# Values' top and remainder side by side in the first attention's loop

## What is computed

```python
q = (xn @ w_q).reshape(B, SQ, 16, 64)
kv = context @ w_kv
k, v = jnp.split(kv, 2, axis=-1)            # each (B, 12544, 16, 64)
scores = jnp.einsum('bqhd,bkhd->bhqk', q * SCALE, k)
attn = jax.nn.softmax(scores, axis=-1)
out = jnp.einsum('bhqk,bkhd->bqhd', attn, v).reshape(B, SQ, 1024)
out = out @ w_out + b_out
return out * jnp.tanh(gate[0])
```

## Time and profile before

| | |
|---|---|
| median of 3 runs | 1176.95 us (1174.17 to 1177.15) |
| profiled execution, its own time | 1175.05 us |
| profiled execution, its span | 1173.3 us |
| busy: PE, DVE, ACT, POOL | 1138.9, 889.1, 901.3, 583.9 us |
| L923, first and last start | 34.6 and 891.9 us |

### The profile page before, as it was taken

How to read it: one execution, slowest core, us unless ns; L and a number is a source line. 1 busy time by engine, 2 the same in 40 slices (tenths; PEclk the granted TensorE clock), 3 DMA queues, 4 the chain that set the end, 5 groups by cost and what they waited for, 6 DMA issues and landing times.

```text
span 1173.3 us, 32542 instructions
## 1 busy us (share of the span) xinstructions
PE 1138.9 (97%) x12748; PEld 814.0 (69%) x12749; DVE 889.1 (76%) x1718; ACT 901.3 (77%) x1552; POOL 583.9 (50%) x548
## 2 busy tenths in 40 slices
PE   8999999999999999999999999999997899889998
PEld 6566666666666666666666666666666758767898
DVE  7777878888888888888878787878774659788632
ACT  5699988889988889898888888889884278586010
POOL 5355656565655565665656565656564070043000
PEclk9999999999999999999999999999999999999999
DMA  5465544445354545354545454544443995150385
GB/s 223 107 183 149 153 116 119 127 95 154 90 154 96 150 92 157 90 154 95 148 95 142 107 138 110 137 108 93 123 92 97 382 341 167 33 180 1 109 285 176
DMA packets 141142, 163.31 MB, mean 139 GB/s; under 512 B 18320, under 2 KB 127280, under 8 KB 140992
## 3 DMA queue, kind: packets, MB, share of 16 engines
q1 hardware_dynamic: 139904, 157.20, 48.0%
q10 hardware_dynamic: 1088, 4.06, 0.9%
HBM read 71.60 MB, written 12.99 MB: 72 GB/s over the span
## 4 chain that ended last, share of the span: by engine, by line
PE 85%; DVE 6%; ACT 4%; issue 2%; DMA 1%; SPq 1%; POOL 0%; DVEq 0%; ACTq 0%; POOLq 0%
PE ps L900 21%; PE ps L872 21%; PE ps L938 7%; PE ps L914 7%; PE ps L2353 4%; PE ps L957 4%; PE ps L955 4%; PE ps L956 4%; PE ps L1681 3%; PE ps L2361 2%; PE ps L1108 2%; ACT ss_decay L1936 2%; PE ps L2135 1%; DMA k_st<-k_rest 1%; PE ps L2117 1%
## 5 line engine op out<-in xcount | busy, mean ns | idle before, releaser
L468 POOL TENSOR_TENSOR pT_lo<-p_exp,pT_hi 128x896 f16<-128x896 f32 x223 | 420.8, 1887 | 313.9 <-ACT pT_hi L580 313.9
L561 ACT ACTIVATE p_exp<-ps,ln_k,esc 128x896 f32<-128x896 f32 x224 | 246.0, 1098 | 54.7 <-PE ps L938 47.1
L693 DVE TENSOR_REDUCE tile_max<-ps 128x128 f16<-128x896 f32 x224 | 244.4, 1091 | 49.6 <-PE ps L914 47.2
L580 ACT ACTIVATE pT_hi<-p_exp 128x896 f16<-128x896 f32 x224 | 211.8, 946 | 1.0
L688 DVE TENSOR_TENSOR v_lo<-ps,v_hi 128x512 f16<-128x512 f32 x196 | 135.4, 691 | 68.6 <-ACT v_hi L553 66.2
L956 PE MATMUL ps<-v_lo,pT_hi 128*128 128x64 f16 x1568 | 164.4, 193 | 0.0
L955 PE MATMUL ps<-v_hi,pT_hi 128*128 128x65 f16 x1568 | 164.3, 193 | 0.1
L957 PE MATMUL ps<-v_hi,pT_lo 128*128 128x65 f16 x1568 | 163.8, 193 | 0.0
L900 PE MATMUL ps<-c_hi,wk_hi 128*128 128x448 f16 x448 | 158.5, 354 | 0.8 <-DVE k_rest L708 0.5
L900 PE MATMUL ps<-c_hi,wk_lo 128*128 128x448 f16 x448 | 157.9, 352 | 0.0
L900 PE MATMUL ps<-c_lo,wk_hi 128*128 128x448 f16 x448 | 157.8, 352 | 0.0
(11 more groups left out here) (406 smaller groups left out, 2074.8 us busy)
## 6 DMA issues: line engine op xcount, KB each, us to landing
k_st<-k_top SPq DMA_DIRECT2D x444, 112.0 KB, 2.3
k_st<-k_rest SPq DMA_DIRECT2D x444, 56.0 KB, 2.0
xa_cn<-in_ctx SPq DMA_DIRECT2D x14, 896.0 KB, 7.5
me_w<-in_me_w SPq DMA_DIRECT2D x8, 1536.0 KB, 6.3
c_raw<-in_ctxT SPq DMA_DIRECT2D x13, 896.0 KB, 5.6
ctx_parts<-c_hi SPq DMA_DIRECT2D x14, 448.0 KB, 3.3
ctx_parts<-c_lo SPq DMA_DIRECT2D x14, 448.0 KB, 2.8
me_w<-in_me_w SPq DMA_DIRECT2D x8, 768.0 KB, 5.9
```

The costliest lines, as they stand in the source:

```text
L468: nc.gpsimd.tensor_tensor(pT_lo[:, n % 2, :, :].rearrange("p t s -> p (t s)"), p_exp[:, n % 2, :], pT_hi[:, n % 2, :, :].rearrange("p t s ...
L561: nc.scalar.activation(p_exp[:, n % 2, :], s_scores[n % 2], ACT.Exp, bias=ln_k[:, 0:1], scale=esc[:, n // H0 % 2:n // H0 % 2 + 1]).then_in ...
L580: nc.scalar.activation(pT_hi[:, n % 2, :, :].rearrange("p t s -> p (t s)"), p_exp[:, n % 2, :], ACT.Copy).then_inc(pT_hi_ready, 1)
L693: nc.vector.tensor_reduce(tile_max[:, n % 2, :], s_scores[n % 2].rearrange("p (t s) -> p s t", s=S), AX.X, ALU.max).then_inc(tile_max_done, 1)
```

## The change

`v_hi` and `v_lo` become one tensor `v_pair`: for each tile and head 64 columns of remainders, 64 of tops, and the ones. `weigh` multiplies `pT_hi` by all 129 columns in one matmul, and `pT_lo` by the last 65 in a second; the third is gone. A head's sum now takes 129 columns of PSUM, so four heads fill the end of bank 6 and the beginning of bank 7, and there is one such place in the stead of two. `flush` has a third operation, which adds the columns of the remainders after the tops, and stands ahead of `v_low` and `tiles_max` in all four steps. `weigh` of the first head of a group waits for the flush of the whole group before (`flushed`), not of the one before that. The transposed maxima go to other columns, without a wait for a flush. The quarters of the next chunk's split move: on ACT from steps 2, 3, 5, 6 to 1, 2, 4, 6, on DVE from 3, 4, 6, 7 to 2, 3, 6, 8 (in chunk 0 ACT keeps its steps, and DVE has 3, 4, 6, 8). SP loads `c_raw` in step 9.

```diff
-VW = DH + 2
+VW = 2 * DH + 2
+V_LO, V_HI = slice(0, DH), slice(DH, 2 * DH)
+PV = 2 * DH + 1
+FLUSH = 3
...
-C_SPLIT_STEPS = (2, 3, 5, 6)
+C_HIGH_STEPS, C_HIGH_FIRST = (1, 2, 4, 6), (2, 3, 5, 6)
+C_LOW_STEPS, C_LOW_FIRST = (2, 3, 6, 8), (3, 4, 6, 8)
...
-        s_pv = [ps[:, b, 0:4 * (DH + 1)].rearrange("p (h e) -> p h e", e=DH + 1) for b in (7, 6)]
+        s_pv = flat[:, 7 * 512 - 2 * PV:7 * 512 + 2 * PV].rearrange("p (h e) -> p h e", e=PV)
...
-                if h == 8 and c + 2 < NCH:
+                if h == 9 and c + 2 < NCH:
                     sp.wait_ge(c_lo_ready, 4 * (c + 2))
                     sp.dma_start(c_raw[:, :, :], ctxT[:, :, (c + 2) * CH:(c + 3) * CH]).then_inc(raw_loaded, 16)
...
-                if h in C_SPLIT_STEPS and c + 1 < NCH:
-                    c_high(c + 1, C_SPLIT_STEPS.index(h))
+                steps = C_HIGH_STEPS if c else C_HIGH_FIRST
+                if h in steps and c + 1 < NCH:
+                    c_high(c + 1, steps.index(h))
...
-                nc.vector.scalar_tensor_tensor(out=acc[:, 4 * g:4 * g + 4, 0:DH], in0=s_pv[g % 2][:, :, 0:DH],
-                                               scalar=v_unscale[:, c % 2:c % 2 + 1], in1=acc[:, 4 * g:4 * g + 4, 0:DH],
-                                               op0=ALU.mult, op1=ALU.add).then_inc(flushed, 1)
-                nc.vector.tensor_tensor(acc[:, 4 * g:4 * g + 4, DH:DH + 1], acc[:, 4 * g:4 * g + 4, DH:DH + 1],
-                                        s_pv[g % 2][:, :, DH:DH + 1], ALU.add).then_inc(flushed, 1)
+                grp = acc[:, 4 * g:4 * g + 4, :]
+                nc.vector.scalar_tensor_tensor(out=grp[:, :, 0:DH], in0=s_pv[:, :, V_HI], scalar=v_unscale[:, c % 2:c % 2 + 1],
+                                               in1=grp[:, :, 0:DH], op0=ALU.mult, op1=ALU.add).then_inc(flushed, 1)
+                nc.vector.tensor_tensor(grp[:, :, DH:DH + 1], grp[:, :, DH:DH + 1],
+                                        s_pv[:, :, 2 * DH:PV], ALU.add).then_inc(flushed, 1)
+                v.wait_ge(flushed, FLUSH * f + 1)
+                nc.vector.scalar_tensor_tensor(out=grp[:, :, 0:DH], in0=s_pv[:, :, V_LO], scalar=v_unscale[:, c % 2:c % 2 + 1],
+                                               in1=grp[:, :, 0:DH], op0=ALU.mult, op1=ALU.add).then_inc(flushed, 1)
                 if c == NCH - 1:
                     hs = slice(4 * g, 4 * g + 4)
-                    v.wait_ge(flushed, 2 * f + 2)
+                    v.wait_ge(flushed, FLUSH * f + FLUSH)
...
+                if h % 4 == 1 and n > 1:
+                    flush(n // 4 - 1)
                 if n and v_at(n - 1):
                     v_low(*v_at(n - 1))
-                if h % 8 == 1 and n > 1:
-                    flush(n // 4 - 1)
                 if n + 2 < NT:
                     tiles_max(n + 2)
-                if h % 8 == 5:
-                    flush(n // 4 - 1)
                 if n + K_AHEAD < NT:
                     k_low(n + K_AHEAD)
-                if h - 1 in C_SPLIT_STEPS and c + 1 < NCH:
-                    c_low(c + 1, C_SPLIT_STEPS.index(h - 1))
+                steps = C_LOW_STEPS if c else C_LOW_FIRST
+                if h in steps and c + 1 < NCH:
+                    c_low(c + 1, steps.index(h))
...
                 if h % 4 == 0:
-                    at_least(pe, flushed, 2 * (c * 4 + h // 4 - 1))
+                    at_least(pe, flushed, FLUSH * (c * 4 + h // 4))
...
-                to = s_pv[h // 4 % 2][:, h % 4, :]
+                to = s_pv[:, h % 4, :]
                 for tile in range(TILES):
                     ph, pl = pT_hi[:, n % 2, tile, :], pT_lo[:, n % 2, tile, :]
-                    nc.tensor.matmul(to, ph, v_hi[:, tile, h, 0:DH + 1], start=(tile == 0), stop=False)
-                    nc.tensor.matmul(to[:, 0:DH], ph, v_lo[:, tile, h, 0:DH], start=False, stop=False)
-                    mm = nc.tensor.matmul(to, pl, v_hi[:, tile, h, 0:DH + 1], start=False, stop=(tile == TILES - 1))
+                    nc.tensor.matmul(to, ph, v_pair[:, tile, h, 0:PV], start=(tile == 0), stop=False)
+                    mm = nc.tensor.matmul(to[:, DH:PV], pl, v_pair[:, tile, h, DH:PV], start=False, stop=(tile == TILES - 1))
```

More of the change, by code:

```diff
@@ L196, in first_cross_attention @@
         esc, m_per, v_unscale = t("esc", [P, 2]), t("m_per", [P, 2]), t("v_unscale", [P, 2])
-        v_hi = t("v_hi", [P, TILES, H0, VW], F16)
-        v_lo = t("v_lo", [P, TILES, H0, VW], F16)
+        v_pair = t("v_pair", [P, TILES, H0, VW], F16)
         p_exp = t("p_exp", [P, 2, CH])
@@ L230, in first_cross_attention @@
         s_max = [flat[:, CH:1024], flat[:, 1024 + CH:2048]]
-        s_pv = [ps[:, b, 0:4 * (DH + 1)].rearrange("p (h e) -> p h e", e=DH + 1) for b in (7, 6)]
-        s_total = ps[:, 6, 304:316]
+        s_pv = flat[:, 7 * 512 - 2 * PV:7 * 512 + 2 * PV].rearrange("p (h e) -> p h e", e=PV)
+        s_total = ps[:, 6, 200:212]
         raw_loaded, ident_ready = sem("raw_loaded"), sem("ident_ready")
@@ L312, in s_turned @@
                 return s_max[1]
[L313 to L316, removed]
+            return ps[:, 6, 0:S] if n % 2 else ps[:, 7, 384:512]
         O_TURNS = (range(0, 4), range(4, 6), range(6, 8))
@@ L418, in _ @@
             nc.gpsimd.memset(run_max[:, 1, :], -BIG).then_inc(ones_ready, 1)
-            nc.gpsimd.memset(v_hi[:, :, :, DH:VW], 1.0).then_inc(ones_ready, 1)
+            nc.gpsimd.memset(v_pair[:, :, :, 2 * DH:VW], 1.0).then_inc(ones_ready, 1)
             pool.wait_ge(ones_ready, 5)
@@ L490, in _ @@
                     pool.wait_ge(decay_ready, f + 1)
-                    at_least(pool, flushed, 2 * (f - 3))
+                    at_least(pool, flushed, FLUSH * (f - 3))
                     grp = acc[:, 4 * g:4 * g + 4, :]
@@ L552, in v_high @@
                     at_least(act, pv_done, c * H0 - (8 if half == 0 else 0))
-                nc.scalar.activation(v_hi[:, tile, 8 * half:8 * half + 8, 0:DH],
+                nc.scalar.activation(v_pair[:, tile, 8 * half:8 * half + 8, V_HI],
                                      v_bank(vn).rearrange("p (h e) -> p h e", e=DH), ACT.Copy).then_inc(v_hi_ready, 1)
@@ L687, in v_low @@
                 v.wait_ge(v_hi_ready, vn + 1)
-                nc.vector.tensor_tensor(v_lo[:, tile, 8 * half:8 * half + 8, 0:DH], v_bank(vn).rearrange("p (h e) -> p h e", e=DH),
-                                        v_hi[:, tile, 8 * half:8 * half + 8, 0:DH], ALU.subtract).then_inc(v_ready, 1)
+                nc.vector.tensor_tensor(v_pair[:, tile, 8 * half:8 * half + 8, V_LO], v_bank(vn).rearrange("p (h e) -> p h e", e=DH),
+                                        v_pair[:, tile, 8 * half:8 * half + 8, V_HI], ALU.subtract).then_inc(v_ready, 1)
             def tiles_max(n):
@@ L919, in turn_max @@
                 pe.wait_ge(tile_max_done, n + 1)
-                if n > 2:
-                    first, f = (n - 2) % 4 == 0, (n - 2) // 4
-                    at_least(pe, flushed, 2 * (f - 1 if first else f))
                 nc.tensor.matmul(s_turned(n), tile_max[:, n % 2, :], ident16[:, :], start=True, stop=True, skip_group_check=True).then_inc(max_turned, 1)
@@ L1094, in _ @@
             spin(nc, spare, ident, 2)
-            keep_warm(nc, pe, spare, ident, flushed, 8 * NCH - 1, 8 * NCH - 1, 2)
+            keep_warm(nc, pe, spare, ident, flushed, 4 * FLUSH * NCH - 1, 4 * FLUSH * NCH - 1, 2)
             keep_warm(nc, pe, spare, ident, rec_ready, 4, 4)
```

## The result

| | before | after |
|---|---|---|
| median of 11 runs | 1175.65 us | 1178.86 us |
| profiled execution, span | 1173.3 us | 1178.0 us |
| ratio of the runs, 95% interval | | 1.0029 (1.0021 to 1.0038) |

The changed kernel is slower by 3.2 us. Of the 4.1 us between 1183 and 1178.86, 1.3 come from the start: the median of 3 runs of the kernel before was 1176.95, that of 11 is 1175.65. The profiled executions are 4.7 us apart, more than the medians, since that of the changed kernel (1179.75) lies .9 over its median and that of the kernel before (1175.05) .6 under its own.

A forecast was written before the change was run, and what follows sets the result against it. PE was taken to bound the loop, with ACT and DVE just in time. Two new waits less the matmul gain, with the remaining terms, made +6.0 us: from the median of 1176.95 to 1183, range 1176 to 1190 (8 in 10).

The forecast's parts named there:

- Price one: ACT's quarter in step 1 delays q_low, so PE's second pass in step 2 waits: .34 us per chunk.
- Price two: In step 9, weigh waits for the flush behind c_lo, starting .54 us later; net .41 per chunk.
- the relief in step 10: PE's .10 us wait for k_low in step 10 goes away, as k_low is delayed less than PE.
- What moves at no cost: SP's later c_raw load in step 9 and turn_max without its flush wait were taken to change nothing.
- The gain: One matmul less per tile in weigh: .03 us per step where PE sets the length, .33 per chunk.
- c_abs's delay of the flush: Behind absmax, step 13 may lose some .05 us waiting for the flush.
- the end: After the last head the flush's third operation and its wait stand in the open: +.45 us.
- chunk 13: The last chunk has seven gaining steps: -.2 us.
- The sum of 6.05: All gains and waits over all chunks and the end, together given as +6.0 us.
- both waits: PE waits for q_low in step 2 and for the flush in step 9; 58%, 1180 to 1187 us.
- one wait does not come: Rival: the flush is over in time or ACT catches up; 1177 to 1180 us, 17%.

The follow-up runs named there:

- high_back: The changed kernel with ACT's quarters back in steps 2, 3, 5, 6 and DVE's in 3, 4, 6, 8: 1174.96 us, ratio .9998.
- split_alone: The kernel before with only the quarters in their new steps and c_raw loaded in step 9: 1178.78 us, ratio 1.0036.
- raw_nine: The kernel before with c_raw loaded in step 9 instead of step 8, nothing else: 1173.3 us, ratio .9986.
- three_matmuls: The changed kernel with pT_hi multiplied by tops and remainders in two matmuls again: 1183.17 us, ratio 1.0068.

## Why the prediction was off in size

Term by term, the working against the changed kernel's steps:

- **Price one** was right: .34 per chunk in step 2, measured .37; with chunk 1's two steps 4.7 in the sum and 5.2 measured. Most of the .03 that it fell short in each step stood in the rows: a second pass that has waited is followed by the next turn after 1.70 (115.57 to 117.27), one that has not after 1.68 (606.86 to 608.54). high_back removes the wait, and split_alone brings it alone. The sum L646 of the earlier trace rows was a true precedent for it.
- **Price two** was right in place and mechanism, but mis-sized: c_lo would "hold DVE for .94". The row behind that is of step 7. In step 8 c_lo holds DVE for .68 (635.22 to 635.90), since pT_lo starts 1.71 after the turn there (633.61, turn 631.90) and 1.97 after it in step 7 before (626.32, turn 624.35), where a c_hi ahead of pT_hi delays it. Against that, PE followed .11 behind the flush, where .05 was taken. The step grew by .31 instead of .51, and the relief in step 10 was .13 instead of .10: .18 a chunk for .41, 2.75 us for 5.3. This is the largest error. Only in chunk 0, where c_lo takes 1.11, did step 9 grow by about what was worked out, .57. It was readable before: c_lo's four places had lengths from 1.01 to 1.11, and it always ended .48 behind the end of pT_lo. The assumed .48 of the third operation, for which the trace before had no row, held.
- **What moves at no cost** is where the second error lies: SP's load of c_raw was put down as worth nothing. It was asked whether the load comes too late, and not what it had stood ahead of. Taken off step 8's keys it gives 1.6 us, as raw_nine shows; the waits behind its new place took .5 of that back in the profiled execution. `turn_max`'s old wait for a flush was not always over either. In step 13 of chunk 13 it stood .3, as the rows behind this list show.
- **The gain** was taken too high: .03 a step, measured about .02 (.2 to .3 us over 13 chunks for each place). The pair gave the .60 that was worked out, and three_matmuls puts it at .03 within one layout; what was not seen is the .01 that goes with the new layout. Steps 0 and 8 gained .3 us each, where the working had them wait for `k_low` anyway. The other steps gave 2.4 us, with the gains inside steps 12 and 13 about 2.9, for 4.3. This error goes the other way, and hides 1.4 us of the two above.
- Small ones: step 13 +.5, of which c_abs's delay of the flush was foreseen as .05 and is .07 before the step's own gain; the end +.6 for .45; chunk 13 -.6 for -.2, of which -.3 is the wait of `turn_max`.

The wait of `turn_max` in step 13 of chunk 13, before:

```profile
891.65 0.15 DVE L721 TENSOR_TENSOR acc<-acc,ps 128x4 f32<-128x4 f32 x1
...
891.95 0.22 PE L923 MATMUL ps<-ident,tile_max 128*128 128x128 f16 x1
```

The turn comes .15 after the end of this flush, which its code has it wait for, and .69 after the start of the second pass (891.26). In the changed kernel, without the wait, it comes .40 after it (895.67 to 896.07). three_matmuls has the shorter step too, and split_alone, which keeps the wait, the longer one.

The sum of 6.05 becomes 4.7 by these. The runs' medians show 3.2; the other 1.5 us is how far the two profiled executions stand from their medians, within a scatter of single executions from 1173.3 to 1177.15 before and 1177.9 to 1179.8 after. The mechanism was right, then: both waits came where they were put. The sum came as near as it did because its errors partly cancel: price two and c_raw put it 4.2 us too high, the gain, price one and the waits in steps 12 and 13 some 3 us too low. Of the rivals, that one wait does not come (1177 to 1180) holds the measured time, though both came.

## What to carry to other kernels

When an instruction is moved, read its length at its new place's neighbours, not at the old ones: here it depended on when another engine's work ended. Work that is moved into a short step pushes the next step's work by its whole length, on an engine with idle time in the mean. And a transfer that moves later gives something to all that was queued behind it; ask what it had stood ahead of, and what it stands ahead of now.

## What the runs showed of the hardware

- DVE's c_lo, with two inputs in SBUF, ends .48 after POOL's pT_lo or .68 after its own start, whichever is later. This holds to .01 for the 520 remainders in the loops of the ten traces; they take .67 to 1.12.
- PE starts .05 after q_low ends (610.49 to 610.54), but .11 after the flush ends in step 9 (637.16 to 637.27). Why the two differ is not known.
- 129 columns in one matmul instead of 65 and 64 in two saved .03 us in 21 matmuls within the same layout (three_matmuls), that is 4 to 5 ns for each one that is gone.
